# Second attention's queries by pairs of batches, its first maximum beside them, and an earlier transposition of half a norm

## The reference

```
x = layer_norm(x + ff, ln_g, ln_b)            # last norm of the first block
h = layernorm(x, gamma, beta)                 # norm ahead of the second attention
Q = (h @ Wq)  K = (context @ Wk)  V = (context @ Wv)      # 16 heads of 64
attn = softmax(Q K^T) * 64 ** -0.5
out  = x + (attn V) @ Wo + bo
```

## Time and profile before

| what | value |
|---|---|
| median of 3 runs | 1022.93 us (1021.35 to 1025.42) |
| the profiled execution, its time | 1023.64 us |
| the profiled execution, its span | 1021.9 us |
| mean granted clock of TensorE over the span | 0.978 of full |
| PE / DVE / ACT / POOL busy | 95% / 71% / 57% / 46% |
| middle block, queries from the first matmul to the last low part | 468.2 to 505.2 us |
| first scores of the last block | 508.35 us |

### The profile page before, as it was taken

One profiled execution on the slowest core, in us unless ns is written; L12 is line 12 of the kernel. 1 busy time (PEld: TensorE's weight loads), 2 busy tenths in 40 slices (PEclk: granted clock), 3 DMA queues, 4 the chain that ended last, 5 costly groups with the idle time before them and its releaser, 6 DMA issues. The chain is left out here.

```text
span 1021.9 us, 28256 instructions
## 1 busy us (share of the span) xinstructions
PE 967.6 (95%) x11977; PEld 708.4 (69%) x11977; DVE 729.2 (71%) x1360; ACT 580.4 (57%) x1162; POOL 471.5 (46%) x349
## 2 busy tenths in 40 slices
PE   6978989999999999896799999999999999999999
PEld 3645667777777776654377777777777777777787
DVE  5767768888888886476667767677676767767752
ACT  2626657777778777666545544455444454445543
POOL 5573322453353213045665545555455554555543
PEclk9978989999999999999899999999999999999999
DMA  3726989899999942200202112022110221202100
GB/s 107 192 70 158 192 177 204 173 192 190 182 196 192 187 117 78 72 1 1 81 28 61 60 44 58 24 63 61 42 60 24 63 61 42 60 24 63 38 4 4
DMA packets 96785, 93.15 MB, mean 91 GB/s; under 512 B 54674, under 2 KB 81508, under 8 KB 96660
## 3 DMA queue, kind: packets, MB, share of 16 engines
q1 hardware_dynamic: 96660, 91.35, 38.7%
HBM read 51.15 MB, written 22.18 MB: 72 GB/s over the span
## 5 line engine op out<-in xcount | busy, mean ns | idle before, releaser
L1803 ACT ACTIVATE P<-PS 125x448 f32<-125x448 f32 x384 | 209.0, 544 | 266.0 <-PE PS L1693 264.1
L1672 POOL TENSOR_TENSOR Pl<-P 125x896 f16<-125x896 f32 x128 | 230.3, 1803 | 238.2 <-ACT P L1803 238.2
L1170 DVE TENSOR_REDUCE m<-PS 128x1 f32<-128x500 f32 x336 | 220.6, 675 | 117.5 <-PE PS L1161 113.9
L1035 DVE TENSOR_REDUCE m_part<-PS 128x1 f32<-128x500 f32 x336 | 214.0, 676 | 49.2 <-PE PS L906 46.8
L1010 ACT ACTIVATE Pb<-PS 125x448 f32<-125x448 f32 x384 | 186.7, 548 | 50.9 <-PE PS L832 50.6
L1709 PE MATMUL PS<-cNh,P 125*128 125x97 f16 x1344 | 197.9, 208 | 0.1
L1711 PE MATMUL PS<-cNh,Pl 125*128 125x97 f16 x1344 | 197.4, 207 | 0.0
L1710 PE MATMUL PS<-cNl,P 125*128 125x96 f16 x1344 | 196.8, 206 | 0.0
L1710 PEld LDWEIGHTS PS<-cNl,P 125*128 125x128 bf16 x1344 | 131.8, 98 | 25.5
L1709 PEld LDWEIGHTS PS<-cNh,P 125*128 125x128 bf16 x1344 | 131.2, 98 | 15.7 <-issue 3.2
L1691 PE MATMUL PS<-Qh,cTh 110*125 110x448 f16 x384 | 138.7, 361 | 1.3 <-DVE Qh L1899 1.3
(11 more groups left out here) (222 smaller groups left out, 1552.5 us busy)
## 6 DMA issues: line engine op xcount, KB each, us to landing
Kst<-k_halves SPq DMA_DIRECT2D x144, 125.0 KB, 3.0
k_halves<-KH SPq DMA_DIRECT2D x16, 750.0 KB, 4.6
cx<-in_ctx SPq DMA_DIRECT2D x32, 281.2 KB
d_cx<-in_ctx SPq DMA_DIRECT2D x16, 562.5 KB
c_halves<-cHi SPq DMA_DIRECT2D x16, 288.0 KB, 6.5
c_halves<-cLo SPq DMA_DIRECT2D x16, 288.0 KB, 8.1
cTh<-c_halves SPq DMA_DIRECT2D x16, 288.0 KB, 3.2
cTl<-c_halves SPq DMA_DIRECT2D x16, 288.0 KB, 4.4
```

The source lines that it names most:

```text
L1035: nc.vector.tensor_reduce(m_part[:, t, part:part + 1], PS[:, 6 + k % 2, 0:SP], AX.X, ALU.max).then_inc(s_reduced, 1)
L1170: nc.vector.tensor_reduce(m21[:, t, part:part + 1], PS[:, S1[k % 2], 0:SP], AX.X, ALU.max).then_inc(n_red, 1)
L1672: nc.gpsimd.tensor_tensor(Pl[:, c % NP], P1[:, c % NP], high, ALU.subtract).then_inc(n_low_p, 1)
L1803: nc.scalar.activation(P1[:, c % NP, half * HALF:(half + 1) * HALF], PS[0:KC, u % 3, 0:HALF], ACT.Exp).then_inc(n_exp, 1)
```

## The change

1. A bank of queries no longer holds one head of a half but four heads of one tile (two batches): bank n is tile n // 4 and heads 4 (n % 4) to 4 (n % 4) + 3. It takes twelve matmuls of 112 columns (three per head). After four banks batches 0 and 1 have all heads, so SP's loads wait for four high parts and four of GpSimd's low parts.
2. `LOW_ON_DVE` has 12 of 32 banks instead of 8: none ahead of 5.
3. The score pieces of the first batch stand at n = 9 to 21: one each at 9 to 12, two each at 13 to 20, one at 21. On DVE the reductions from n = 9 on stand behind `normalise(1)`, and `turned_low(1, 2)` stands behind those of n = 15.
4. The first maximum's chain moves into the middle block: DVE negates it at n = 24, PE transposes it there into bank 4 behind its 25th bank of queries, DVE lays it at n = 25. PE, ACT and DVE lose their first pass of the last block.
5. ACT rounds the first context in the middle block, behind `keep_turned_weights(act, 2, ...)`.
6. `turn(0)` moves ahead of `third_layer(1)` on PE, `keep_turned(0)` ahead of both `high_of_product` on ACT, `turned_low(0)` ahead of both `low_of_product` on DVE.

```diff
+        def negate_maximum(dve, n):
+            dve.wait_ge(n_red, n * 21 + 21)
+            nc.vector.tensor_reduce(mt1[:], m21[:], AX.X, ALU.max).then_inc(n_mlink, 1)
...
+        def lay_maximum(dve, n, bank):
+            dve.wait_ge(n_mturned, n + 1)
...
-        LOW_ON_DVE = (1, 4, 7, 10, 13, 18, 23, 28)
+        LOW_ON_DVE = (5, 7, 10, 12, 15, 17, 20, 22, 24, 26, 28, 30)
+        MAX_BANK = 4
+        BESIDE_QUERIES = beside(0, (0,) * 9 + (1,) * 4 + (2,) * 8 + (1,) + (0,) * 10)
+        FIRST_MAX = 24
...
-        def pieces_beside(n):
-
-            return range(min(2 * max(n - H - 4, 0), NPC), min(2 * max(n - H - 3, 0), NPC))
+        def pair_of(n):
+
+            t, g = divmod(n, 4)
+            return slice(2 * t, 2 * t + 2), slice(4 * g, 4 * g + 4)
...
-                load_halves(sp, -1, 1, 0, ((g_high, H),))
-                load_halves(sp, -1, 1, 1, ((g_low, lows_by(True, H)), (g_low_p, lows_by(False, H))))
+                load_halves(sp, -1, 1, 0, ((g_high, 4),))
+                load_halves(sp, -1, 1, 1, ((g_low_p, 4),))
...
-                    o = PS[0:DC, QK_BANKS[n % 5], 0:HALF]
-                    pe.matmul(o, Wqk16[:, 0, h, :], Thi[:, cols], start=True, stop=False)
...
+                    for j in range(4):
+                        h, o = 4 * g + j, PS[0:DC, QK_BANKS[n % 5], 0:HALF].rearrange("p (b h q) -> p b h q", b=2, h=4)[:, :, j, :]
+                        pe.matmul(o, Wqk16[:, 0, h, :], Thi[:, cols].rearrange("p (b q) -> p b q", b=2), start=True, stop=False)
+                        pe.matmul(o, Wqk16[:, 1, h, :], Thi[:, cols].rearrange("p (b q) -> p b q", b=2), start=False, stop=False)
+                        if n % H == 0 and j == 0:
+                            pe.wait_ge(t_low, half + 3)
+                        mm = pe.matmul(o, Wqk16[:, 0, h, :], Tlo[:, cols].rearrange("p (b q) -> p b q", b=2), start=False, stop=True)
+                    mm.then_inc(g_made, 1)
...
                 values_by_outputs(0)
+                turn(0, TURN2_BANK, e_normed)
                 third_layer(1)
                 values_by_outputs(1)
-                turn(0, TURN2_BANK, e_normed)
                 for n in range(2 * H):
                     if n == H - 2:
+                        pe.wait_ge(t_full, 3)
                         turn(1, TURN2_BANK, e_normed)
                     queries(n)
-                    for k in pieces_beside(n):
+                    for k in BESIDE_QUERIES[n]:
                         score_piece1(pe, -1, 1, k)
+                    if n == FIRST_MAX:
+                        pe.wait_ge(n_mready, 1)
+                        pe.wait_ge(t_full, 4)
+                        pe.matmul(PS[96:96 + MR, MAX_BANK, 0:128], mn1[:], ident, start=True, stop=True).then_inc(n_mturned, 1)
...
                 keep_turned_weights(act, 2, WvT, WVT_BANKS)
+                act.wait_ge(n_cx[0], 16)
+                nc.scalar.copy(cNh[:, 0, :, 0:DC], d_cx[:, 0]).then_inc(n_cn, 1)
                 for m in range(1, 4):
                     keep_layer(1, 1, m)
+                keep_turned(0, TURN2_BANK, 2)
                 high_of_product(0, WVO_BANKS, wvo_made, Wvo16, D, wvo_high)
                 high_of_product(1, WVO_BANKS, wvo_made, Wvo16, D, wvo_high)
-                keep_turned(0, TURN2_BANK, 2)
...
-                queries_low(1)
                 statistics(1, X, d_link[1], 13, each=1)
                 variance(1, e_link[1], 4, e_var)
-                queries_low(4)
+                queries_low(5)
                 queries_low(7)
                 normalise(1, X, e_root, e_normed)
-                queries_low(10)
-                queries_low(13)
-                turned_low(1, 2)
-                for n in range(H, 2 * H):
+                for n in range(8, 2 * H):
+                    if n == H:
+                        turned_low(1, 2)
                     queries_low(n)
-                    for k in pieces_beside(n):
+                    for k in BESIDE_QUERIES[n]:
                         reduce_piece1(dve, -1, 1, k)
+                    if n == FIRST_MAX:
+                        negate_maximum(dve, 0)
+                    if n == FIRST_MAX + 1:
+                        lay_maximum(dve, 0, MAX_BANK)
...
-                over_pairs(pe, body, before=((-1, 1),))
+                over_pairs(pe, body)
...
-                over_pairs(act, body, before=((-1, 1),))
+                over_pairs(act, body)
...
-                over_pairs(dve, body, before=((-1, 1),))
+                over_pairs(dve, body)
```

More of the change, by code:

```diff
@@ L1170, in reduce_piece1 @@
             nc.vector.tensor_reduce(m21[:, t, part:part + 1], PS[:, S1[k % 2], 0:SP], AX.X, ALU.max).then_inc(n_red, 1)
+        mt1 = sb_in(late, "mt1", [128, QT])
+        mh1 = sb_in(late, "mh1", [128, QT], F16)
+        mn1 = sb_in(late, "mn1", [128, MR])
+        n_mready, n_mturned, n_mlaid = (sem(n) for n in ("n_mready", "n_mturned", "n_mlaid"))
+        n_cn = sem("n_cn")
+        def negate_maximum(dve, n):
+            dve.wait_ge(n_red, n * 21 + 21)
+            nc.vector.tensor_reduce(mt1[:], m21[:], AX.X, ALU.max).then_inc(n_mlink, 1)
+            dve.wait_ge(n_mlink, n * 3 + 1)
+            nc.vector.tensor_scalar(mt1[:], mt1[:], -LIFT, None, ALU.add).then_inc(n_mlink, 1)
+            dve.wait_ge(n_mlink, n * 3 + 2)
+            nc.vector.tensor_copy(mh1[:], mt1[:]).then_inc(n_mlink, 1)
+            dve.wait_ge(n_mlink, n * 3 + 3)
+            wait_for(dve, n_mturned, n)
+            nc.vector.tensor_scalar(mn1[:, 0:QT], mh1[:], -1.0, None, ALU.mult)
+            nc.vector.tensor_tensor(mn1[:, QT:], mh1[:], mt1[:], ALU.subtract).then_inc(n_mready, 1)
+        def lay_maximum(dve, n, bank):
+            dve.wait_ge(n_mturned, n + 1)
+            nc.vector.tensor_tensor(Qh[96:96 + MR, n % 2].rearrange("p (t q) -> p t q", t=QT),
+                                    spread(PS[96:96 + MR, bank, 0:128], 1, QT),
+                                    spread(tab[96:96 + MR, C_MM:C_M16], 2, 128), ALU.mult).then_inc(n_mlaid, 1)
         Wvo16 = sb_in(late, "Wvo16", [DC, 2, H, D], F16)
@@ L1217, in lows_by, with queries_at @@
             return sum((k in LOW_ON_DVE) == dve for k in range(n))
-        def pieces_beside(n):
-            return range(min(2 * max(n - H - 4, 0), NPC), min(2 * max(n - H - 3, 0), NPC))
+        def pair_of(n):
+            t, g = divmod(n, 4)
+            return slice(2 * t, 2 * t + 2), slice(4 * g, 4 * g + 4)
+        def queries_at(part, n):
+            batches, heads = pair_of(n)
+            return QK[:, part, batches, heads, :].rearrange("p b h q -> p b (h q)")
         def keep_turned_weights(act, which, out_, banks):
@@ L1256, in low @@
                 def low(n):
-                    half, h = divmod(n, H)
                     k = lows_by(False, n)
                     pool.wait_ge(g_full, k + 1)
-                    at = slice(8 * half, 8 * half + 8)
-                    nc.gpsimd.tensor_tensor(QK[:, 1, at, h, :], stage[:, k % NSTAGE].rearrange("p (b q) -> p b q", b=8), QK[:, 0, at, h, :],
+                    nc.gpsimd.tensor_tensor(queries_at(1, n), stage[:, k % NSTAGE].rearrange("p (b c) -> p b c", b=2), queries_at(0, n),
                                             ALU.subtract).then_inc(g_low_p, 1)
@@ L1358, in queries @@
                 def queries(n):
-                    half, h = divmod(n, H)
-                    cols = cols_of(half)
-                    if h == 0:
+                    t, g = divmod(n, 4)
+                    half, cols = t // 4, slice(t * TP, (t + 1) * TP)
+                    if n % H == 0:
                         pe.wait_ge(t_high, half + 3)
@@ L1439, in keep_queries @@
                 def keep_queries(n):
-                    half, h = divmod(n, H)
                     act.wait_ge(g_made, n + 1)
                     o = PS[0:DC, QK_BANKS[n % 5], 0:HALF]
-                    nc.scalar.activation(QK[:, 0, 8 * half:8 * half + 8, h, :], o.rearrange("p (b q) -> p b q", b=8), ACT.Identity,
+                    nc.scalar.activation(queries_at(0, n), o.rearrange("p (b c) -> p b c", b=2), ACT.Identity,
                                          scale=1 / WS).then_inc(g_high, 1)
@@ L1539, in queries_low @@
                     if n in LOW_ON_DVE:
-                        half, h = divmod(n, H)
                         dve.wait_ge(g_high, n + 1)
-                        at = slice(8 * half, 8 * half + 8)
-                        nc.vector.scalar_tensor_tensor(out=QK[:, 1, at, h, :], in0=PS[0:DC, QK_BANKS[n % 5], 0:HALF].rearrange("p (b q) -> p b q", b=8),
-                                                       scalar=1 / WS, in1=QK[:, 0, at, h, :], op0=ALU.mult, op1=ALU.subtract).then_inc(g_low, 1)
+                        nc.vector.scalar_tensor_tensor(out=queries_at(1, n), in0=PS[0:DC, QK_BANKS[n % 5], 0:HALF].rearrange("p (b c) -> p b c", b=2),
+                                                       scalar=1 / WS, in1=queries_at(0, n), op0=ALU.mult, op1=ALU.subtract).then_inc(g_low, 1)
```

(4 more changed lines are left out.)

26 lines of the change are left out of this document (2 added, 24 removed).

## The result

The changed kernel took 1027.78 us (median of 19 runs, 1024.58 to 1032.94), the kernel before 1023.66 beside it (19 runs, 1020.87 to 1028.52). The ratio is 1.0041, with a 95% interval of 1.0026 to 1.0056: some 4.2 us slower. The time lies above the predicted range of 1018.2 to 1025.8 us. Of the runs beside the experiments two, one of e6 (1104.27 us) and one of the kernel before (3321.46 us), were disturbed, and no ratio counts them.

The account below looks back on a forecast made before the run. PE, busy 95% of the span, was taken as the bound, so the last block's first scores and their clock decide. +1.35 us later start and -1.9 us from full clock gave -0.55, hence 1022.4 us; 8-in-10 range 1018.2 to 1025.8.

Parts of the forecast that it names:

- The front: First half's transposition goes ahead of the third layer; bank 0 filled at 466.4 instead of 468.24, 1.8 us sooner.
- Cost nothing: Price put on moving the first half's transposition into PE's 2.90 us wait ahead of the third layer.
- Fills 0 to 11: ACT bounds these banks, bank 11 kept at 476.5; root ends at 476.2, `normalise(1)` at 479.6 instead of 481.5.
- The stop of over 5 us: Behind fill 11 PE waits at piece 2 for the first reduction, 474.9 to 480.4, 5.5 us, then half clock.
- Reductions: DVE from 479.6: 16.6 us of work plus waits, sum 19.6; last reduction ends at 499.2 instead of 503.0.
- The maximum and the tail: PE waits for the maximum behind fill 24, then ACT needs 4.7 us; first scores at 509.7, 1.35 us later.
- Sum: Whole kernel: +1.35 us for later first scores, -1.9 us for full clock, together -0.55 us.
- The head: Last block, first scores to GpSimd's second context rest (`cNl`, batch 1): full clock there gains 1.9 us.
- Packed: Faster rival, chance 0.2: normalise not held up by POOL, PE warm, waits vanish, maximum hidden; 1018, or 1019.5 with two.
- Cold: Slower rival, chance 0.15: stops leave PE cold at the first scores, only +1.35 us left; 1024.3 us.
- Late: Rival, chance 0.05: no overlap, first maximum late, pieces standing behind load or norm longer than computed; 1025 us.

Follow-up runs that it names:

- e6: Changed kernel with root first, maximum's transposition four banks later, turned rest sooner, and GpSimd's low parts waiting for the second half's norm; 1017.51 us, 0.9934 of before.
- e2: Kernel before with only the first half's transposition, its evictions and its low part moved ahead; 0.9996 of before.
- e3: Changed kernel with the root of the second half's last norm ahead of all low parts on GpSimd; 1.0002 of before.
- e11: Changed kernel run again, nothing altered; 1.0037 of before.
- e12: e6 run again, nothing altered; 0.9933 of before.
- e9: Kernel before with only the maximum's chain in the middle block and ScalarE rounding the first context in the feed-forward; 0.9995 of before.
- e4: Changed kernel with TensorE's transposition of the maximum four banks later, behind bank 28 instead of 24, and the laying at 29; 0.9994 of before.

## Why the prediction was wrong

**The front: the position right, the price wrong.** Bank 0 was forecast to be filled at 466.4, rel 6.9, and ACT to keep it at rel 8.0. In after they are at 463.62 and 464.71, rel 6.9 and 8.0. The first step that failed is "Cost nothing". I had followed the moved work on PE, ACT and DVE, but not what it pulls along: POOL's low 0 starts at 465.96, rel 9.3 (forecast 9.5), and six of them run in a row beside six of the eight instructions of `with_gain(1)`. The prediction quoted the Trainium skill, "SBUF — State Buffer", section "Who interferes with whom", and applied it to the four normalising instructions alone. The trace shows the same for six of the eight `scalar_tensor_tensor` ahead of them, whose two tensor inputs both lie in SBUF: 0.28 us each becomes 1.06, the time of one low part. By that section of the Trainium skill a VectorE instruction with two SBUF inputs contends with a GpSimd instruction that reads SBUF. The trace agrees, and e2 and e3 show it from either side. Price in after: 4.7 us of DVE. Only 1.1 us of it shows against the forecast of the norm's end, since the forecast had the root wait for six low parts anyway.

**Fills 0 to 11.** The root was forecast behind six lows, ending at rel 16.7. It ended at 475.37, rel 18.7, held up by DVE. The norm beside two lows took 2.55 us (forecast 3.4 with three) and ended at rel 21.2, against 20.1. The stop of over 5 us that I placed at piece 2 became 4.17 us at bank 10, for low 5: it stands on DVE behind `with_gain(1)`, and the forecast didn't ask when it would be done. The place is wrong, the price nearly right, and half clock followed as forecast (0.52).

**Reductions.** Forecast rel 39.7, measured 41.5: 1.1 from the late norm, 0.7 of waits. The stop at bank 16 for `turned_low(1, 2)` was in the sum with 1.05 us; it was 2.42 on PE, and the 4 us behind it ran at 0.58. That half clock wasn't in the sum at all.

**The maximum and the tail.** The stop of PE was forecast as some 2.2 us and measured as 2.33. The second step that failed is the tail behind it: I priced it as ACT's eleven operations at 0.43, 4.7 us, "PE alone would need 7 x 0.59 = 4.1 us, so it isn't the bound". The forecast took full clock there. The matmuls behind the stop start 0.094 us apart from 502.40 to 505.76, 1.12 us a bank; up to there PE is the bound and ACT waits for it. From there on PE is at full clock again and ACT is the bound. From 502.92 to 508.97 the tail took 6.05 us. ACT, timeline:

```profile
502.92 0.54 ACT L1479 ACTIVATE QK<-PS 96x448 f16<-96x448 f32 x1 [2.83 <-PE PS L1410]
...
505.16 0.54 ACT L1479 ACTIVATE QK<-PS 96x448 f16<-96x448 f32 x1 [0.58 <-PE PS L1410]
```

The prediction took half clock to follow pauses of 3.6 us and more, and full clock pauses of 2.9 and less. Here it followed pauses of 2.4 and 2.3 us among other short ones, and in e11 one of 1.6 us behind which after ran at full clock. The length of one pause wasn't a usable rule: one kernel with one pause gave either clock, and what decides stays open.

**Sum.** Of the 3.6 us by which the first scores came later than forecast (rel 53.9 against 50.2), 1.1 are the norm's, 0.7 more waits up to the last reduction, 0.4 more up to the first bank behind the maximum, and 1.35 the tail at half clock (6.05 against 4.7). Behind POOL's last low part everything was as forecast: 0.5 us to the first scores (0.4), a pause of 2.73 us, full clock. The head took 11.8 us instead of 13.85, a gain of 2.06 for which 1.9 had been taken. That gives +5.0 - 2.1 = +2.9 us at the second `cNl`, where -0.55 had been forecast. The head's gain was in part luck: it came in after and e11, but e6 and e12 show that the pause of 2.73 us doesn't bring it each time.

**The runs.** The means of the 19 runs each differ by 3.9 us (1028.35 and 1024.46). Over all executions of the kernels here the time goes with the mean granted clock by about -0.70 us for each 0.001 (correlation -0.82 within the kernels). Brought by that to the same clock of 0.978, after stands at 1027.1 and before, with its runs beside the experiments, at 1024.1: 3.0 us of schedule, close to the 2.9 of the trace, and the rest, about 1 us, is more half clock (mean clock 0.9762 in after, 0.9772 in before). This split rests on a correlation, and the 2.9 hold some half clock themselves. Where the 1 us lies isn't shown. The third layer is one candidate: it ran at half clock in four of the ten traces with edit 6 and in none of the three without it.

**The rivals.** "Packed" named the right lever, a norm that isn't held up by POOL, but the change did the opposite; e6 is what packed meant. It said 1018 for the change and e6 took 1017.5; that the two are so close is chance. "Cold" was wrong in its place: not the scores were cold, but the tail. "Late" came nearest, 1025 with a chance of 0.05: pieces behind the norm longer than computed. It was underrated because only one collision of DVE and POOL had been priced.

## What to carry to other kernels

When a step is moved forward, list what becomes ready sooner because of it, down to the last queue, and ask beside which instructions it now runs: here a transposition that itself cost nothing put GpSimd's low parts over eight VectorE instructions on the way to the bottleneck. If such a pair collides, let the engine with slack wait: 2 us of an idle GpSimd bought 1.9 us at the block's end. And a step that waits in the middle of PE's fixed list cost the wait here and half clock behind it; put it some banks behind the point at which its input is there.

## What was not expected of the hardware

VectorE's `scalar_tensor_tensor` on 112 x 128 with both tensor inputs in SBUF took 0.28 us alone and 1.06 in step with GpSimd's subtraction of 1.03 us. Even instructions of seven columns, a `tensor_scalar` and a cast, pay the whole of it: 0.97 instead of 0.17 us in e9, 1.03 in e4:

```profile
503.06 1.03 DVE L1183 CAST mh<-mt 128x7 f16<-128x7 f32 x1
```

A chain with such tiny instructions should therefore be counted by the low parts it may meet, not by its own 0.9 us.
